# Score matmuls of a half first and side by side, max matmuls behind them, turns next to the value products

## The reference

```
xn = layernorm(x)
zn = layernorm(xn) * ln_w + ln_b
q, k, v = split(zn @ W_qkv + b_qkv)            # 16 heads of 8
attn = softmax(q @ k.T / sqrt(8))              # per sequence and head, 1024 x 1024
s = xn + (attn @ v) @ W_proj + b_proj
logits = xn @ Wr + br; weights = softmax over the top 2 experts
f = sum_e weights_e * (gelu(xn @ W1_e + b1_e) @ W2_e + b2_e)
out = x + s * silu(f)
```

## Time and profile before

| | |
|---|---|
| median of 3 runs | 1130.09 us (1127.98 to 1131.12) |
| the profiled execution | 1128.22 us, its span 1126.4 us |
| PE busy | 1062.3 us, 94% |
| DVE busy | 882.2 us, 78% |
| ACT busy | 869.9 us, 77% |
| exponentials L787 | 512 of 1023 ns, 500.6 us |
| max reductions L1238 | 768 of 684 ns, 486.4 us |
| value products L982 | 2048 records, 268.4 us |

### The profile page before, as it was taken

One profiled execution on the slowest core, in us unless ns is written; L12 is line 12 of the kernel. 1 busy time (PEld: TensorE's weight loads), 2 busy tenths in 40 slices (PEclk: granted clock), 3 DMA queues, 4 the chain that ended last, 5 costly groups with the idle time before them and its releaser, 6 DMA issues.

```text
span 1126.4 us, 17266 instructions
## 1 busy us (share of the span) xinstructions
PE 1062.3 (94%) x6041; PEld 439.0 (39%) x6041; DVE 882.2 (78%) x1519; ACT 869.9 (77%) x1189; POOL 357.3 (32%) x545
## 2 busy tenths in 40 slices
PE   5999999999999999999999999999999999999995
PEld 3666665556656565663122222212122212212123
DVE  6737777777777687666999999999999999999715
ACT  6876666666767676667889898888888888988982
POOL 4785667566666666452110001000000000000001
PEclk9999999999999999998999999999999999999999
DMA  6432322214131312223211112111211111111102
GB/s 181 120 110 53 101 53 67 79 45 103 31 116 38 106 40 78 60 72 93 55 33 44 45 30 58 31 45 30 58 31 44 44 45 45 30 44 30 31 1 75
DMA packets 84992, 67.42 MB, mean 60 GB/s; under 512 B 9277, under 2 KB 71402, under 8 KB 84906
## 3 DMA queue, kind: packets, MB, share of 16 engines
q1 hardware_dynamic: 84906, 66.32, 21.9%
HBM read 51.08 MB, written 15.20 MB: 59 GB/s over the span
## 4 chain that ended last, share of the span: by engine, by line
PE 53%; ACT 19%; DVE 6%; issue 4%; ACTq 0%; DVEq 0%; POOL 0%; POOLq 0%
ACT p_ring L787 17%; PE psum L982 13%; PE psum L960 11%; PE psum L900 6%; PE psum L865 4%; PE psum L867 3%; PE psum L866 3%; PE psum L881 3%; PE psum L886 2%; PE psum L889 2%; PE psum L887 2%; PE psum L995 2%; DVE neg_max_half L1256 1%; DVE neg_max_half L1238 1%; DVE h_lo L1200 1%
## 5 line engine op out<-in xcount | busy, mean ns | idle before, releaser
L787 ACT ACTIVATE p_ring<-psum 128x1024 f32<-128x1024 f32 x512 | 500.6, 1023 | 66.5 <-PE psum L960 62.7
L1238 DVE TENSOR_REDUCE neg_max_half<-psum 128x1 f32<-128x512 f32 x768 | 486.4, 684 | 38.2 <-PE psum L900 29.4
L900 PE MATMUL psum<-k_max_stack,q_max_stack 48*128 48x512 bf16 x1024 | 300.6, 386 | 18.4 <-DVE neg_max_half L1256 12.3
L960 PE MATMUL psum<-q_stack,k_stack 51*128 51x512 bf16 x1024 | 279.4, 383 | 13.1 <-ACT p_ring L787 4.3
L982 PE MATMUL psum<-p_ring,v_sb 128*9 128x512 f32 x2048 | 268.4, 597 | 0.4 <-ACT o_sb L778 0.4
L750 ACT ACTIVATE h_hi<-psum,cols 128x512 fp32r<-128x512 f32 x192 | 132.6, 690 | 138.3 <-PE psum L867 134.2
L631 POOL TENSOR_TENSOR h_lo<-h_split,h_hi 128x512 fp32r<-128x512 f32 x128 | 165.8, 1300 | 138.8 <-ACT h_split L753 137.2
L1256 DVE TENSOR_REDUCE neg_max_half<-psum 128x2 f32<-128x1024 f32 x128 | 156.5, 1223 | 60.2 <-PE psum L900 59.8
L960 PEld LDWEIGHTS psum<-q_stack,k_stack 51*128 51x128 bf16 x1024 | 60.3, 94 | 306.5 <-ACT p_ring L787 283.0
L581 POOL CAST neg_max_parts<-neg_max_rest 128x16 bf16<-128x16 f32 x32 | 6.9, 214 | 510.8 <-DVE neg_max_rest L1247 510.7
L753 ACT ACTIVATE h_split<-psum,cols 128x512 f32<-128x512 f32 x192 | 131.7, 686 | 0.0
(11 more groups left out here) (119 smaller groups left out, 920.9 us busy)
## 6 DMA issues: line engine op xcount, KB each, us to landing
expert_w_bc<-expert_w_dram SPq DMA_DIRECT2D x64, 256.0 KB, 4.9
k_rows_dram<-qk_parts SPq DMA_DIRECT2D x24, 256.0 KB, 3.0
q_max_stack<-q_rows_dram SPq DMA_DIRECT2D x64, 96.0 KB, 2.5
k_max_stack<-k_rows_dram SPq DMA_DIRECT2D x64, 96.0 KB, 2.5
q_stack<-q_rows_dram SPq DMA_DIRECT2D x64, 96.0 KB, 2.5
k_stack<-k_rows_dram SPq DMA_DIRECT2D x64, 96.0 KB, 2.5
q_rows_dram<-qk_parts SPq DMA_DIRECT2D x8, 384.0 KB, 2.7
xz<-in_L_attn_z_dram SPq DMA_DIRECT2D x8, 256.0 KB, 3.3
```

The costliest lines, as they stand in the source:

```text
L787: act.activation(p_sb[:, n % PR, a, :, :].rearrange("p h t -> p (h t)"), scores_bank[s % 2], ACT.Exp, scale=SCALE).then_inc(S("P"), 1)
L900: return pe.matmul(to, q_m[rows, slot, t * P:(t + 1) * P], k_m[rows, slot, c * TG:(c + 1) * TG], start=True, stop=True)
L960: i = pe.matmul(scores_bank[s % 2][:, hh * TG:(hh + 1) * TG], k_s[rows, slot, kt * P:(kt + 1) * P], q_s[rows, slot, a * TG:(a + 1) * TG], ...
L1238: dve.tensor_reduce(mx[:, p % MXR, c, hh * NT + t:hh * NT + t + 1], ring_bank(("max", u)), AX.X, ALU.max, negate=True).then_inc(S("R"), 1)
```

## The change

A half now issues both score matmuls next to each other, raises ACT's semaphore, and then issues its max matmuls next to each other. The first half of a block takes two max matmuls and the second what is left of the block's three or four (before, 1 or 2 in either half, evenly spread). The turns move from between the halves to behind the second half, next to the value products, on PE, on DVE (`head_out`) and on ACT (the copy of the turned maxima, now behind the second exponential). The order of the items on the ring follows: both halves' max matmuls, then the turns.

```
 def singles_upto(n, half):
-    return min(len(SINGLES), -(-((2 * n + half) * len(SINGLES)) // (2 * MAX_BLOCKS)))
+    upto = [min(len(SINGLES), -(-((n + a) * len(SINGLES)) // MAX_BLOCKS)) for a in range(2)]
+    return (upto[0], min(upto[0] + 2, upto[1]), upto[1])[half]
...
-    for item in halves[0] + turns + halves[1]:
+    for item in halves[0] + halves[1] + turns:
         on_ring(item)
...
     # ACT
-                    if n in turn_at and a == 0:
-                        neg_max_t(turn_at[n])
+                if n in turn_at:
+                    neg_max_t(turn_at[n])
...
     # PE, scores(s, singles)
-    units = [u for _, u in singles]
-    first = 1 - SINGLES[units[0]][3] if units else 0
-    for k, hh in enumerate((first, 1 - first)):
+    for hh in range(2):
         rows = slice(HALF * hh, HALF * hh + SROWS)
         i = pe.matmul(scores_bank[s % 2][:, hh * TG:(hh + 1) * TG], k_s[rows, slot, kt * P:(kt + 1) * P],
                       q_s[rows, slot, a * TG:(a + 1) * TG], start=True, stop=True)
-        if k:
-            i.then_inc(S("S"), 1)
-        for u in units[k::2]:
-            max_scores(u)
+    i.then_inc(S("S"), 1)
+    for _, u in singles:
+        max_scores(u)
...
     # PE, a block
     scores(2 * n, halves[0])
-    for kind, k in turns:
-        m_t(k) if kind == "mT" else o_t(k)
...
     scores(2 * n + 1, halves[1])
+    for kind, k in turns:
+        m_t(k) if kind == "mT" else o_t(k)
     if n > 1:
         pv(n - 2)
...
     # DVE, a block
     for _, u in halves[0]:
         row_max(u)
-    for kind, k in turns:
-        if kind == "oT":
-            head_out(k)
...
     for _, u in halves[1]:
         row_max(u)
+    for kind, k in turns:
+        if kind == "oT":
+            head_out(k)
```

## The result

The changed kernel takes 1144.01 us (median of 4 runs, 1143.12 to 1144.69) against 1130.61 us (4 runs, 1127.98 to 1131.49): a ratio of 1.0122, 95% interval 1.0103 to 1.0142. It is slower by 13.4 us. The forecast was 1143.

The account below looks back on a forecast made before the run. Latencies between engines bound the kernel: ACT waiting for score matmuls, PE for max reductions. Per 40 blocks 93.4 against 91.1 us gave +13.9, with +0.7 behind them 1142.8 from 1128.2; forecast 1143, 8 in 10 within 1130 to 1150.

Parts of the forecast that it names:

- The 40 blocks that repeat: Attention phase: the pattern of block kinds recurs every 40 blocks, 91.1 us before and 93.4 after.
- The sum: 237 blocks, +13.9 us, and +0.7 behind block 240: +14.6 on the profiled execution's 1128.2, giving 1142.8.
- Part 1: Plain blocks: the exponential starts 0.49 behind the score matmuls, not 0.70; a gain of 1.5 us in 40 blocks.
- The loop of two blocks: Plain blocks: a PE and ACT cycle over two blocks falls from 4.21 to 4.00 us, blocks of 1.95 and 2.05.
- Part 2: Blocks with four max matmuls: the first reduction starts later, so they take 2.71 us, with `half_min` 2.86 or 2.78.
- Part 3: Blocks with turns: turns become fourth items and wait for the first reduction; `o_t` 2.98 against 2.69, `m_t` 2.59 against 2.47.
- the double blocks: Blocks with four max matmuls and `o_t`, or both turns: the fifth item waits; 3.58 us each, against 3.08 and 3.23.
- rule on mode changes: Turn next to value products: changing tiling mode drains TensorE, a step of 0.31 rather than 0.20, 5 us more in all.
- A: Blocks with a fourth item: its wait doesn't grow, only the plain blocks' gain of 9 acts, about 1120 us; chance 0.09.
- B: Blocks with a fourth item: half of the ring's 22.6 us growth is hidden, no change, 1131 us; chance 0.10.
- C: Score matmul pairs: the early exponential doesn't come, the gain of 9 is missing, 1152 us; chance 0.07.
- D: Turn blocks: the step from a turn to the value products is 0.31, not 0.20; 5 us more, 1148; chance 0.14.

Follow-up runs that it names:

- the kernel by block: Against the kernel before: score matmuls first only in blocks without a fourth max matmul or a turn, all other blocks as before; 1125.21 us, ratio 0.9955.
- The short reductions: Max reductions read 256 of 512 columns, in the changed kernel (1116.3 us, 0.9886 of the unedited one before) and the one before (1114.4 us, 0.9874).
- turns only: The kernel before with its turns alone moved behind the second half; 1135.93 us, ratio 1.0048.

## Why the prediction was right

**The whole.** The 40 blocks that repeat took 91.05 us before and 93.44 after (blocks 54 to 93, and the repeats behind them alike), against 91.1 and 93.4 worked out. So the mechanism was right, and its size too. That the median came within 1 us of 1143 is partly luck. The sum gave +14.6 on the profiled execution; with the 1.9 by which the median of the runs shown lay higher, it gives 1144.7, and I put 1143 without a reason. The medians differ by 13.4, and the 237 blocks by 13.1 where 13.9 was forecast, in part since blocks 3 and 4, at and behind the low clock, were 0.4 shorter in this execution than in the one before.

**Part 1, score matmuls first.** The loop of two blocks behaved as worked out: exponential 0.49 behind the pair, plain blocks of 1.95 and 2.05, with 2.18 where `o_copy` intervened (767.23 to 769.41 above). That last one I had expected only where `o_copy` stands in a plain block behind another plain one; it also comes behind a long block. The 25 plain blocks of a repeat take 50.23 (forecast 50.1), and took 51.68 before (51.6): a gain of 1.45 against 1.5. The table's means, 2.019 and 2.080, lie 0.015 above what was worked out for either kernel; about 0.01 of that is block 3 at the low clock, without which they are 2.010 and 2.071. The gain in all: 149 x 0.061 = 9.1 us, against 1.5 x 5.9 = 8.9.

**Part 2, max matmuls later.** The reduction starts at +1.62 rather than +1.64, and the block with four takes 2.69, not 2.71. With `half_min` it is 2.76, where I had 2.78 and 2.86: the case that `half_min` delays the first reduction further didn't come true. All 23 take 2.76. DVE's timeline has block 120, whose block ahead was 2.04 long:

```profile
798.89 0.17 DVE L1245 TENSOR_TENSOR neg_max_rest<-neg_max_half 128x16 f32<-128x16 f32 x1
799.09 2.48 DVE L1236 TENSOR_REDUCE neg_max_half<-psum 128x1 f32<-128x512 f32 x4
```

`half_min` stands at +1.50 as forecast, but the first reduction follows 0.20 later, not 0.29: the step in the earlier trace rows that I had taken for its length held some waiting for the max matmul. Even the 0.20 holds some. In block 110, behind an `o_t` block, `half_min` starts at +0.96 and in block 140 at +1.26, and the first reduction still starts at +1.69. In the kernel by block, where the data are there sooner, it starts 0.09 behind the `half_min` at +1.50. So `half_min`'s own delay never decided; the term was 0.06 a block too high on average.

**Part 3, the turns.** `m_t` 2.61 (forecast 2.59), `o_t` 3.02 (2.98), the double blocks 3.62 (3.58). A turn started 2.46 behind the value products (771.36, 773.82), where I had 2.39; a max matmul that waits for the same reduction starts at 2.37 (762.59, 764.96). The step from an `o_t`'s start to the value products is 0.56 (773.82, 774.38), and from `m_t` 0.15 (779.60, 779.75), for which I had put 0.59 and 0.20. The two misses nearly cancel. By the Trainium skill's rule on mode changes (TensorEngine Tiling (Array Packing), Key Properties) I had weighed 0.31 behind the last transposition, in place of the 0.20 in the sum. The trace doesn't show that much: the last transposition of the `o_t` starts 0.20 ahead of the value products (774.18, 774.38), two transpositions 0.11 apart (774.07, 774.18), and `m_t`'s step is 0.15. A drain can be part of these steps, but a small one.

**What decided.** The long blocks cost 22 us and the plain ones gave 9, which is the sum. The short reductions show the sign's cause: with them the same two orders are level. Rivals A (the wait doesn't grow), B (half of it hidden; 22 of the 22.6 us came) and C (no early exponential) are refuted by the rows, D (0.31 from a turn to the value products) by `m_t`'s 0.15 and by an `o_t`'s 0.56 from its start, less than the 0.59 in the sum. One sign was worded wrongly: the waits of PE for max reductions were to rise from 34.2 to 55 or more, and the row that had 34.2 has 42.1; the rest of the growth is in the rows of the matmuls and the turns.

**What stays open.** Why a turn starts 0.09 later behind the reduction that it waits for than a max matmul does (a mode change that begins only once the wait is over would do it; no run separates that); why a first reduction behind `half_min` starts 0.07 later, whenever `half_min` itself stood (in the kernel before too, +1.48 and not +1.41); and whether the 2.7 us ahead of the attention phase are chance alone. The nine profiles scatter enough for it, and two with the same code there differ by 1.9, but no kernel was profiled twice.

## What to carry to other kernels

Where a ring of buffers is shorter than what a stage puts on it, count the items of each stage: the one that needs the stage's own first buffer again sets its length, and what matters then is when the first item is handed over, not when the last is. An instruction brought forward in an in-order queue puts every other one back; it pays in stages that wait for it and costs in those that wait for the one it passed, so choose the order per stage, and look at what a stage leaves late for the next. Judge that by a stage's length in its kinds and not by the mean: here one kind gained 0.06 and the others lost 0.13 to 0.55, and choosing by block kept more than half of the gain (5.3 of 9 us).

## What the runs showed of the hardware

- A max reduction of 512 columns takes 0.69 us alone, and back to back they start 0.60 apart; of 256 columns 0.42, starting 0.33 apart. What another engine waits for is the first number: the fourth max matmul started 0.06 behind the end of a reduction of 0.69.
- A turn next to the value products cost no more than one next to score matmuls: 0.58 from its start to the value products in "turns only", 0.59 to the score matmuls in the kernel before.
- In all nine profiles the granted clock was at 0.50 for a few us around the start of the attention phase. In the kernel before this made block 3 take 3.65 us in place of about 2.
